# Gate products of an LSTM-like recurrence by a seven-product scheme, two row blocks in turn, output head as a last stage

## What is computed

```python
def step(c, xt):                      # xt: 2048 x 512, normalised rows of batch b
    ft = sigmoid(xt @ wf.T + c @ uf.T + bf)
    it = sigmoid(xt @ wi.T + c @ ui.T + bi)
    gt = tanh(xt @ wc.T + c @ uc.T + bc)
    c = ft * c + it * gt
    return (c, None)
c_final, _ = lax.scan(step, c0, x)    # c0: in_c on every row
h = tanh(einsum('tbi,oi->tbo', x, wo) + c_final @ uo.T + bo)
out = x + layernorm(h)
```

## Time and profile before

| what | value |
|---|---|
| median of 3 runs | 2887.04 us |
| the profiled execution: its own time | 2888.32 us |
| its span, first to last instruction | 2886.5 us |
| TensorE, weight loads | 97% and 80% of the span |
| VectorE, ScalarE, GpSimd | 57%, 35%, 27% of the span |
| granted TensorE clock, mean | 0.984 of 2.4 GHz |
| moved by DMA | 308.66 MB, mean 107 GB/s |

### The profile page before, as it was taken

How to read it: one execution, slowest core, us unless ns; L and a number is a source line. 1 busy time by engine, 2 the same in 40 slices (tenths; PEclk the granted TensorE clock), 3 DMA queues, 4 the chain that set the end, 5 groups by cost and what they waited for, 6 DMA issues and landing times.

```text
span 2886.5 us, 57402 instructions
## 1 busy us (share of the span) xinstructions
PE 2786.0 (97%) x23763; PEld 2298.1 (80%) x23763; DVE 1652.6 (57%) x3652; ACT 1005.1 (35%) x2028; POOL 781.5 (27%) x1169
## 2 busy tenths in 40 slices
PE   4599999989999999999999999999999999999998
PEld 4288888878887788788878887888788778878884
DVE  8755555555446645655565556555664565465535
ACT  6655656632223322322233223222322232222223
POOL 7766576411112211221121112211221121121102
PEclk8699999989999999999999999999999999999999
DMA  9878778772322231322232213212222222222201
GB/s 338 284 235 272 273 267 281 273 226 54 65 53 66 60 74 38 77 63 59 38 81 60 59 41 77 74 45 52 70 70 46 54 69 68 49 56 70 67 12 59
DMA packets 404549, 308.66 MB, mean 107 GB/s; under 512 B 274368, under 2 KB 340416, under 8 KB 398016
## 3 DMA queue, kind: packets, MB, share of 16 engines
q1 hardware_dynamic: 404288, 305.00, 37.5%
HBM read 195.88 MB, written 76.02 MB: 94 GB/s over the span
## 4 chain that ended last, share of the span: by engine, by line
PE 91%; DVE 4%; ACT 1%; POOL 1%; issue 1%; DMA 1%; SPq 0%; DVEq 0%; POOLq 0%; ACTq 0%
PE bank L1478 35%; PE bank L1489 30%; PE bank L1517 10%; PE bank L1383 3%; PE bank L1333 3%; PE bank L1369 3%; PE bank L1391 2%; PE bank L1345 1%; PE bank L1504 1%; DVE big L1058 1%; PE bank L1353 1%; DVE big L1133 1%; DMA big<-yd 0%; ACT big L896 0%; DMA big<-xr 0%
## 5 line engine op out<-in xcount | busy, mean ns | idle before, releaser
L1478 PE MATMUL bank<-big 128*128 128x256 f16 x9216 | 1039.1, 273 | 2.3 <-DVE big L1176 1.5
L1478 PEld LDWEIGHTS bank<-big 128*128 128x128 f16 x9216 | 902.5, 98 | 126.2 <-DVE big L1176 1.8
L1489 PE MATMUL bank<-big 128*128 128x256 f16 x8064 | 911.2, 273 | 0.0
L1489 PEld LDWEIGHTS bank<-big 128*128 128x128 f16 x8064 | 789.0, 98 | 95.8
L882 ACT ACTIVATE big<-bank,big 128x256 f32<-128x256 f32 x768 | 402.5, 561 | 1145.8 <-PE bank L1489 1128.9
L1205 DVE TENSOR_TENSOR big<-big 128x256 f32<-128x256 f32 x224 | 94.9, 423 | 574.4 <-ACT big L882 572.0
L1517 PE MATMUL bank<-big 128*128 128x512 f16 x1536 | 348.8, 379 | 0.0
L1517 PEld LDWEIGHTS bank<-big 128*128 128x128 f16 x1536 | 150.3, 98 | 160.3
L689 POOL TENSOR_SCALAR big<-big 128x1 f32<-128x1 f32 x128 | 33.1, 258 | 797.4 <-DVE big L1157 795.9
L704 POOL TENSOR_SCALAR big<-big 128x1 f32<-128x1 f32 x128 | 28.0, 219 | 796.8 <-DVE big L1236 796.8
L889 ACT ACTIVATE big<-big 128x512 f32<-128x512 f32 x128 | 80.6, 630 | 465.4 <-DVE big L1232 465.4
(11 more groups left out here) (188 smaller groups left out, 2832.7 us busy)
## 6 DMA issues: line engine op xcount, KB each, us to landing
big<-xr SPq DMA_DIRECT2D x16, 2048.0 KB, 11.0
big<-xg SPq DMA_DIRECT2D x64, 512.0 KB, 6.8
big<-kpad SPq DMA_DIRECT2D x32, 1024.0 KB, 12.3
yd<-big SPq DMA_DIRECT2D x16, 2048.0 KB, 17.4
big<-x SPq DMA_DIRECT2D x64, 512.0 KB, 6.0
out<-big SPq DMA_DIRECT2D x128, 256.0 KB, 2.0
big<-yd SPq DMA_DIRECT2D x62, 512.0 KB, 6.7
big<-wts SPq DMA_DIRECT2D x16, 1024.0 KB, 9.5
```

Source lines behind the costliest of these rows:

```text
L1478: ins = e.matmul(gate_out(m, g), W[2 * g][:, lw, kt, m * 128:(m + 1) * 128], src[:, lx, kt, :], start=(n == 0 and g != 1), stop=last, skip ...
L1489: ins = e.matmul(gate_out(m, g), W[2 * g + 1][:, lw, kt, m * 128:(m + 1) * 128], src[:, lx, kt, :], start=False, stop=(n == 11), skip_grou ...
```

## The change

The recurrence is cut anew. A **unit** is 512 rows of one batch (32 units u); two quarters of the 2048 rows run in turn, so unit u needs the state of unit u - 2. A group n (192 of them, six per unit) is one gate g and one index a: it makes all four quadrants (two row halves by two output halves) of 128 outputs each. The 2 x 2 block product of rows and weights is made by a seven-product scheme of Strassen's kind in the form with shared partial sums. The sums of weight quarters are made once in the first stage (steps "sum", "hi", "lo": seven quarters per matrix where four stood, for the six gate matrices), the sums of row quarters by DVE per unit (row_sums), the sums of state quarters too (state_sums). Each product is 2 slices of depth x 3 pairs of parts, with the rows and again with the state: 6 or 12 matmuls of 256 columns. Products 1, 4, 2, 5 are written first, ACT copies three partial results into an SBUF tile zt in between (k6, k5, ka), the later products 7, 3, 6 are accumulated on what was copied, and DVE adds the two banks to zt (u1, u2). Sigmoid and tanh then read zt.

The prepared rows of a unit (8 items: for each row half two halves of the features as they are and two sums) are transposed by DMA, 16 transposes per unit, the first unit's too. The sum with x (x1) and the transposed rows are stored to DRAM (x1d, xtd), the final states too (cfd), and the head runs after the recurrence as a stage of its own: 4 x (4 last-state products + 32 heads), for which rows are loaded back. The initial state's product is made on DVE in the first stage ("start", twelve instructions) and kept in accd. yd's layout is changed from (group, t, k, b, h) to (group, t, b, k, h).

```diff
+PROD = {1: (0, 0, 0, 0), 2: (1, 0, 2, 1), 3: (2, 3, 2, 6), 4: (6, 1, 2, 2), 5: (3, 2, 0, 3), 6: (4, 2, 2, 4), 7: (5, 3, 0, 5)}
+def unit(u):
+    return u % 16 // 2, 2 * (u // 16) + u % 2
...
 def prep_schedule():
+    at = {g: [] for g in range(GROUPS + 5)}
+    for v in range(1, NU):
+        if v <= 3:
+            places = [6 * (v - 1) + r for r in range(6)]
+        elif v <= 6:
+            first = 18 + 5 * (v - 4)
+            places = [first, first + 1, first + 2, first + 3, first + 4, first + 4]
+        else:
+            places = [6 * v - 9 + r for r in range(6)]
...
+            elif n < 12:
+                places = [("sum", r, n, 7 + r) for r in range(4)]
+                places += [("hi", q, n, 7 + q) for q in range(7)]
+                places += [("lo", q, n, (9, 11, 12, 13, 14, 15, 15)[q]) for q in range(7)]
```

On SyncE, the loads and transposes of a unit and the beginning of the second stage:

```diff
+            def load_y(v):
...
+                w.wait_ge(s["ss"], 8 * v)
+                w.wait_ge(s["xh"], 8 * v - 2)
+                w.wait_ge(s["xlo"], 8 * v - 2)
+                e.dma_start(yt, src).then_inc(s["yl"], 16)
...
+            def prepare(stage, v):
+                if stage == 2:
+                    store_x1(v, 0)
+                    store_x1(v, 1)
+                if stage == 3:
+                    store_x1(v, 2)
+                if stage == 4:
+                    store_x1(v, 3)
+                    turn(8 * v)
+                    turn(8 * v + 1)
+                if stage == 5:
+                    for k in range(2, 6):
+                        turn(8 * v + k)
+                    if v + 1 < NU:
+                        load_x1(v + 1, 0)
+                        load_x1(v + 1, 2)
+                if stage == 6:
+                    if v + 1 < NU:
+                        load_y(v + 1)
+                    turn(8 * v + 6)
+                    turn(8 * v + 7)
+                    if v + 1 < NU:
+                        load_x1(v + 1, 1)
+                        load_x1(v + 1, 3)
+                    store_xt(v)
...
+            w.wait_ge(s["cv"], G * (NG - 1))
+            load_y(0)
+            for c in CHUNKS:
+                load_x1(0, c)
             store_y(NG - 2)
+            load_WX(4)
+            load_WX(5)
...
+                load_WC(n)
             store_y(NG - 1)
...
+            load_WC(5)
+            for stage in range(1, 7):
+                prepare(stage, 0)
```

On ScalarE, in each iteration n of the groups, with pieces of the preparation and of the state's high parts between the lines:

```diff
+                    w.wait_ge(s["p6"], n)
+                    e.activation(zt[(n - 1) % 3][:, 1, :], bank_a(n - 1)[:, 0:256], ACT.Copy).then_inc(s["k6"], 1)
...
+                    w.wait_ge(s["pb"], n + 1)
+                    e.activation(zt[n % 3][:, 3, :], bank_b(n)[:, 256:512], ACT.Copy).then_inc(s["k5"], 1)
...
+                    w.wait_ge(s["pa"], n + 1)
+                    e.activation(zt[n % 3][:, 0::2, :], bank_a(n)[:, :].rearrange("p (q t) -> p q t", q=2), ACT.Copy).then_inc(s["ka"], 1)
...
+                if 1 <= n <= GROUPS:
+                    gates(n - 1)
```

On VectorE, in each iteration n:

```diff
+                    w.wait_ge(s["p3"], n)
+                    w.wait_ge(s["k6"], n)
+                    z = zt[(n - 1) % 3]
+                    e.tensor_tensor(z[:, 0:2, :], bank_b(n - 1)[:, :].rearrange("p (q t) -> p q t", q=2), z[:, 0:2, :], ADD).then_inc(s["u1"], 1)
+                if u and 1 <= gi <= 3:
+                    state_sums(u - 1, gi - 1)
+                for stage, v in PREP_AT[n]:
+                    prepare(0, stage, v)
+                if 1 <= n <= GROUPS:
+                    w.wait_ge(s["p7"], n)
+                    e.tensor_tensor(z[:, 2:4, :], bank_a(n - 1)[:, 0:256].unsqueeze(1).to_broadcast([128, 2, 256]), z[:, 2:4, :], ADD).then_inc(s["u2"], 1)
+                for stage, v in PREP_AT[n]:
+                    prepare(1, stage, v)
+                if 1 <= n <= GROUPS:
+                    gates(n - 1)
```

On TensorE, the inner loops of a product, the order of the products and the head's loop:

```diff
+                for kt in range(2):
+                    for lw, lx in PARTS:
...
+                        ins = e.matmul(o, WX[2 * g + lw][:, q, kt, 128 * a:128 * a + 128], slot[u % 2][:, part, lx, k0 + kt, :],
...
+            for n in range(GROUPS + 1):
+                if n < GROUPS:
+                    A, Bn = bank_a(n), bank_b(n)
+                    if n >= 4:
+                        w.wait_ge(s["u1"], n - 3)
+                    product(n, 2, Bn[:, 0:256], True)
+                    product(n, 5, Bn[:, 256:512], False, "pb")
+                    if n >= 4:
+                        w.wait_ge(s["u2"], n - 3)
+                    product(n, 4, A[:, 256:512], True)
+                    product(n, 1, A[:, 0:256], False, "pa")
+                if n:
+                    w.wait_ge(s["k6"], n)
+                    product(n - 1, 7, bank_a(n - 1)[:, 0:256], False, "p7")
+                if n < GROUPS:
+                    w.wait_ge(s["k5"], n + 1)
+                    product(n, 3, Bn[:, 256:512], False, "p3")
+                    w.wait_ge(s["ka"], n + 1)
+                    product(n, 6, A[:, 0:256], False, "p6")
...
+            for h in range(128):
+                if h % 32 == 0:
+                    last_state(h // 32)
```

More of the change, by code:

```diff
@@ new lines, in sync_program @@
+            e.dma_start(Wo, wd[0]).then_inc(s["wu"], 16)
+            for r in range(NXR):
+                load_xt(r)
+            for h in range(5):
+                load_rb(h)
+            for h in range(128):
+                j, v, c, _ = head_at(h)
+                b = unit(v)[0]
+                w.wait_ge(s["hres"], h + 1)
+                e.dma_start(out[b, 512 * j + 128 * c:512 * j + 128 * c + 128, :], rb[h % NRB]).then_inc(s[f"rb{h % NRB}"], 16)
+                if h + 5 < 128:
+                    load_rb(h + 5)
+                if h % 2 and h // 2 + NXR < 64:
+                    load_xt(h // 2 + NXR)
+                if h == 4:
+                    load_last(1)
@@ L1184, in first_unit @@
-            def first_unit(bi, stages):
-                for stage in stages:
-                    for cc in range(2):
-                        prep(stage, 2 * bi + cc)
-            first_unit(0, ("stat", "add", "norm", "part"))
-            w.wait_ge(s["fb"], 12)
-            w.wait_ge(s["w_scl"], 4)
-            for g in range(3):
-                b0().scalar_tensor_tensor(bias0[:, g, :], bank[6][:, g * 4:g * 4 + 4], inv[g], bias[:, g, :], MUL, ADD).then_inc(s["b0"], 1)
-            first_unit(1, ("stat", "add", "norm", "part"))
@@ L1546, in pe_program @@
-            last_state(7)
-            for n in range(18):
-                head(7, n)
+            w.wait_ge(s["gl"], 8 * NG)
+            w.wait_ge(s["stlo"], 15 * NG)
+            w.wait_ge(s["omlo"], piece_base(NG))
+            w.wait_ge(s["w_scl"], 4)
+            w.wait_ge(s["accs"], 16 * 4)
+            for g in range(3):
+                for m in range(4):
+                    e.matmul(bank[6][:, 4 * g + m:4 * g + m + 1], fbs[:, g, 128 * m:128 * m + 128], one[:, 0:1], start=True, stop=True).then_inc(s["fb"], 1)
```

1094 lines of the change are left out of this document (629 added, 465 removed), and 4 rows, old and new, of the table names.

## The result

The changed kernel takes 2892.02 us (median of 20 runs, 2881.32 to 2900.04), the kernel before 2886.97 us (20 runs, 2885.41 to 2888.06). The ratio is 1.0016, 95% interval 1.0009 to 1.0024: no difference, or 0.2% slower. The forecast was 2794 us, its range 2735 to 2865. Its sign was wrong, and it was 98 us too low.

A forecast was written before the change was run, and what follows sets the result against it. TensorE's number of matmuls was taken to bound the second stage; -235.9 + 10 + 62 + 16 + 12 + 35 + 5 + 3 = -92.9 us took the span from 2886.5 to 2793.6, forecast 2794 us, range 2735 to 2865.

The forecast's parts named there:

- Products removed, -235.9: Gate matmuls fall from 17280 to 15120; 2160 fewer at 109.2 ns each save 235.9 us.
- First stage, +5: VectorE's added 39.7 us and ScalarE's 12.9 find room before the recurrence; +5 us, between 0 and 40.
- The start, +35: Unit 0's transposes queue on SP behind stores and loads; product 5 runs at 644 to 646 instead of 611.2.
- Units without a state, +62: Units 0, 1, 16, 17: VectorE becomes the bound, 163.9 us against TensorE's 110.1, plus about 8 us.
- 12 for load_y: Units 16 and 17: the next unit's statistics wait for load_y, 24 us after stage 5 against 14 to 17.
- Borders of units 2 to 4, +10.4: Waits for late DMA transposes: 6 us at unit 2, 2.4 and 2 at units 3 and 4.
- the margin of gi = 1: Units with a state: the fullest group has 0.4 us margin, once per unit; 0.4 x 26 = +10 us taken.
- The head, +3: Head as its own stage stays 373 us, a head per 2.59 us; only the end is later, +3 us.
- signs of being wrong: TensorE busy under 97% between 900 and 1400 us, clock below 1.0 in stateless units, or head DMA share at 1.
- transfers late: Rival, chance 0.15: load_y lands in 10 to 13 us, or head transfers are slow; time 2825 to 2875.
- Half clock: Rival, chance 0.07: 24 stateless groups run matmuls at 218 ns, 9.2 us instead of 7.2; +48, 2842 us.
- The chance of 0.12 for slower: Overall chance of slower; its rival (0.10) has TensorE waiting in every group of units with a state, 2945 us.

The follow-up runs named there:

- e4: Changed kernel with the load of the next unit's y issued from ScalarE in stage 6 instead of SyncE's queue: 2839.9 us, ratio 0.9841.
- e12: Changed kernel with y's load from ScalarE, start loads reordered, GpSimd's normalisations in quarters and preparation ahead from unit 4 on: 2797.5 us, ratio 0.9688.
- e15: As e11, and from the second matrix on all seven low parts are a memset of one column, high parts in full: 2858.0 us.
- e14: As e11, and from the second matrix on the three further parts of each, high and low, are reduced to one column: 2873.1 us.
- e11: Changed kernel without the 24 weight differences, their parts cut from the plain quarters: 2870.7 us.
- e2: Changed kernel with SyncE loading accd right after the first y and the six later weights after the first unit's preparation: 2880.7 us, ratio 0.9981.
- e1: Changed kernel with the 24 weight differences and the 12 starting-product instructions shrunk to one column, parts cut from plain quarters: 2876.1 us.

## Why the prediction was wrong

The sum's own steps, from the profile and the runs. By the marks on TensorE's timeline the first stage is 40 us over its term, the start 9, and all behind product 5 48: the 98 us of the span.

- *Products removed, -235.9.* Right. 15120 matmuls, and 55.0 us per unit in e4 and e12, to the decimal.
- *First stage, +5.* **Failed, measured +45.** The count of instructions was right; two things in the step were not. Their duration was taken from rows in which GpSimd was idle or did not meet them: 39.7 us were forecast and VectorE took 80.2 more than before, the gap being 26 us in the weight differences (1.83 us each for 0.73), 11 in the five low parts that were held and 4 in the starting product. And their room was counted by the engine's busy share ("107 of 200"), so that 5 of 39.7 us should show; in the runs 0.4 to 0.6 of VectorE's added time does, held or not (e15, e14, e11). At that rate even unheld instructions would have cost 16 to 24 us, an estimate. The argument that 64 instructions already stood there at no cost looked at kinds that were not held: half were reductions with one SBUF input (27 of 32 start inside a normalisation in the changed kernel and take 0.68 us like the others), and none of the 32 low parts met GpSimd; why not, no run shows. The Trainium skill (SBUF — State Buffer, "SBUF: two separate sides") says that VectorE in a two-port mode, or with two inputs in SBUF against a GpSimd instruction that reads SBUF, and GpSimd take a pair of ports as an exclusive lock for the whole instruction. By that rule the trace agrees, down to the two-element instructions of 1.56 us on average. The prediction did not weigh it.
- *The start, +35.* Measured +44.2; +30.5 with the loads in another order (e2). The step that failed is the queue ahead of the transposes: the text lists stores of y, weights and accd, and not the four stores of x1, in which SyncE stood 27.1 us and for whose landing VectorE's row sums waited 12.39. By the forecast SyncE would be free at 621, with the first stage's delay of 45 at 666; the first transposes came at 675.6, and at 660.2 in e2. The 12.7 us in which TensorE waited for accd lay beside this.
- *Units without a state, +62, with 6 at unit 1's border and 12 for load_y.* Near in size, and the mechanism is not borne out: their excess over the bare products is 92.6 us against 80; with y on time (e4) it is 76.6 against 68, the sum without load_y. But VectorE, which the step has as their bound, is busy 64 to 79% of them in e4. Two of its four windows, units 1 and 17 (columns as in the earlier trace rows):

```profile
745.80:801.30 55.50, 38.03 (x285) 29.33 (x284) 38.53 (x66) 29.58 (x53) 10.67 (x24) 0.85 0.43 114
1637.98:1686.63 48.65, 34.75 (x277) 28.08 (x275) 38.64 (x68) 29.54 (x54) 10.89 (x26) 0.89 0.54 133
```

No engine fills these units. TensorE waits 30.3 us in units 0 and 1 of e4, 17.5 of them for transposes, and 25.0 in units 16 and 17, all for ScalarE's copies k6, k5 and ka; the tie of TensorE to those copies is as the step has it. The rest, 12 and 9 us, is TensorE busy for longer than the bare products need, at granted clocks of 0.85 to 0.89. That the sum came near is in part luck.
- *Borders of units 2 to 4, +10.4, and +0.4 per unit with a state.* **Failed.** Units 2 to 5 had 37.4 us of excess, the 22 later ones 18.5. The sum charges the wait of the statistics for load_y in units 16 and 17 only; in units with a state the text lets the queue bear it. But it named who waits for the load and not what is queued behind the waiting instruction: ScalarE, in order, stood in L1017 with k6 behind it. e4, which moves this load and nothing else, takes away 52 us, and the margin of gi = 1 then costs nothing (55.0). What stays in units 2 to 5 (24.8 us) goes to 12.8 when the preparation is ahead from unit 4 on (e12), which is the size forecast.
- *The head, +3.* Right: 100% busy, DMA share 0.78, a head each 2.59 us, VectorE in the tail each 2.76.

Two of the text's own signs of being wrong came: TensorE was busy 474.4 of 500 us between 900 and 1400 (95%, under the 97), and the clock fell below 1.0 in the stateless units. Of the rivals, *transfers late* named the right load and the wrong reason: it priced a longer landing (10 to 13 us), and y landed in 7.3; what was late was its issue. *Half clock* came in part: the granted clock was 0.82 and 0.83 in the windows of the stateless units and 0.93 in those behind them. In those four units TensorE was busy 139.5 us for bare products of 117.9, so matmuls drawn out at the lower clock come to about 22 us (an estimate) where the rival had 48; no run changed the clock alone. The sign was wrong because of what the first stage and the units cost over their terms, 40 and 48 us, most of it on engines that the profile shows half idle; the two together are all but 5 us of the forecast gain of 93, and the start brings 9 more. The chance of 0.12 for slower rested on chains per group, which did not come.

## What to carry to other kernels

Where a step is moved or a load put in a queue, ask what stands behind the first instruction that waits for it on each in-order engine, and follow that to the engine that sets the time; room in the preparation does not help if the critical copies queue behind it. A duration of a VectorE instruction with two SBUF inputs holds only for stretches in which GpSimd does as little as in the row it was read from. Cutting GpSimd's instructions in halves brought 16 us here without taking any work off VectorE, and leaving out the 24 differences, most of them held, 21. An instruction that is being held can't be priced by shrinking it: leave it out. And an engine's idle half is no room for instructions that stand in front of a chain: about half of what VectorE took on came out as delay.

## What the runs showed of the hardware that was not expected

- A VectorE instruction of 512 columns with both inputs in SBUF that starts inside a GpSimd normalisation ends about 0.55 us after that one's end: 1.6 to 2.9 us for 0.67 to 0.75. With two elements per partition it ends 0.02 us after it and still takes 1.56 us on average (e1). A TENSOR_SCALAR with one SBUF input was held too (2.61 us for 0.48), a TENSOR_REDUCE with one was not (0.68 beside GpSimd or not), and an instruction that reads PSUM and SBUF keeps its 0.41 us beside the same GpSimd work.
- It goes both ways: the normalisation takes 2.40 us alone and 2.56 to 2.86 us beside such instructions of VectorE.
- In the kernel before, halving GpSimd's instructions made VectorE's low parts longer (743 to 813 ns on average, three of 32 now met GpSimd) and the kernel 3 us slower: a profile in which two engines do not meet says little of what a small shift brings.
